# Delta rule on one core: key scaling after the value scaling, eight attention tiles, and loads at other places of SyncE's order

## The chip, the cores and the metric

The kernel runs on one core of a Trainium2 chip. The metric is the device time of one execution in microseconds: 3272.89 us is the median of three runs of the kernel before (3272.14 to 3275.28). The core has TensorE (PE: matmuls, and PEld for its weight loads), VectorE (DVE), ScalarE (ACT), GpSimd (POOL), and SyncE (SP), which here only issues transfers. Each engine works through its own instructions in the order in which they are written, and waits at an instruction until the semaphores it names have reached their values.

## The reference, cut to what matters

Two transformer layers. The change lies in the first one's attention, a gated delta rule over 1024 tokens, 2 sequences, 16 key heads and 32 value heads of 128:

```
q, k, v = silu(conv4(hidden @ W_qkvz));  q, k = l2norm(q) / sqrt(128), l2norm(k)
for each token:                       # per sequence and value head
    S = S * exp(g)
    delta = (v - k @ S) * beta
    S = S + outer(k, delta)
    o = q @ S
out = norm(o * silu(z)) * norm_w @ W_out
```

All else (the routed feed-forward layer before it in the program, the second layer after it) is untouched.

## The kernel before

`delta_rule` computes the scan in chunks of 128 tokens. One *step* is one key head and one chunk, for both sequences and both value heads of the key head (U = 4 units): 16 heads by 8 chunks, 128 steps. Within a chunk the triangular system of the delta rule is solved through the inverse of a 128 by 128 matrix, which is built from inverses of 16 by 16 blocks on GpSimd (`base_start`, `base_row`), doubled on TensorE.

The steps run in a software pipeline. A *slot* is one pass through `body` on each engine; in slot s an engine works on step s minus a lag for each function: `S_P` = 0 (projections, convolution), `S_S` = 1 (SiLU), `S_F` = 2 (keys' transposes, decay matrix, N, attention), `S_L` = 5, `S_D` = 6 (state, solve, apply), `S_E` = 7 (output). `t.c` is the chunk of a step, s its number, so an even slot has even `t.c` at lag 0. The functions of a slot stand in a fixed order written out by hand in each engine's `body`, and none is skipped over: a wait in one holds all that stand behind it on that engine. Between engines only semaphores order the work.

What the text below speaks of, by engine:

- ScalarE: `ztanh`, `expo` (L878, the decay matrix ET from rowb), `norms`, `silu`, `from_state`, `normed` (L963, output scaled, waits for GpSimd's `out_scale`), `xev64` (L933), `wev64` (L941), `kdec` (L888, keys scaled into kd), `vscale` (L900, values scaled into vb), `evac(0)`, `clamp` (L866, Relu on rowb for the next slot's `expo`), `evac(1)` (L923, L924), `gtev`, `squares`.
- TensorE, in this order: keys' transposes, state, `w3`, `x16` (reads Tp), `causal`, `w1` (reads Wp), `x64` (L607), first half of projection 0, `w64` (L620, waits for `xev64`), `w2`, `solve` (L710, waits for `wev64`), second half of projection 0, `values` (L659), `apply` (L721 with kd, L724 with attn), projection 1 (L681, waits for `vscale` of this slot, which frees its bank), `gated_tp`, `zproj`, `project_out`.
- VectorE: among others `strict` (L1138, N), `uscale`, `attention` (L1151), `update`, `output`, `taps` (L1193).
- GpSimd: `step_gates`, `causal` (L417), `derive` (L401 to L408), `halo`, `base_rest` (even slots: rows 6 to 14 of the block inverses), `base_first` (odd slots: `base_start` L459, then rows 1 to 5 by L471 and L475), `out_scale` (L442 to L450).
- SyncE: `decays` (L304, loads rowb, once this slot's `expo` has read the old one), `weights`, `base_out` (even slots: blk_t, blk_w out, Tp, Wp back in), `dump` (L346 writes N to DRAM; in odd slots it then waits for that write and issues L351, the load of Bk, the blocks that `base_start` of the same slot waits for).

kd, attn, N and vb are rings of four tiles. So `kdec` of step s-2 overwrites the kd of step s-6, which is read in this very slot by L721, and waits for it. `attention` stands in the same relation to L724:

```
wait(act, up_mm, t.done(RING))     # kdec
wait(dve, au_mm, t.done(RING))     # attention
```

In `base_start` the wait for Bk, with `read` the count of all loads up to this pair of steps:

```
read, sent = held(pool, t.pairs(16, 16)), held(pool, t.pairs(16))
pool.wait_ge(m["made"], 2)
pool.wait_ge(blk_in, read)
```

Of the kernel before, what the change touches and what calls it, by code (L numbers as in the profile page):

```python
# [11 lines left out]
P = 128  # L12
# [6 lines left out]
U = 4  # L19
# [89 lines left out]
def delta_rule(nc, ins, m, l2, hd, acc, xn, xnT, gates, rows):  # L109
# [7 lines left out]
    with ExitStack() as ctx:  # L117
# [15 lines left out]
        rowb = [sb(f"rowb{r}", [P, U, P]) for r in range(2)]  # L133
        ET = sb("ET", [P, U, P])
        N = [sb(f"N{r}", [P, U, P]) for r in range(RING)]
        attn = [sb(f"attn{r}", [P, U, P]) for r in range(RING)]
        kd = [sb(f"kd{r}", [P, U, P]) for r in range(RING)]
        vb = [sb(f"vb{r}", [P, U, P]) for r in range(RING)]

# [88 lines left out]
        def held(eng, val):  # L228

            if not isinstance(val, int):  # L230
                eng.to_reg(val)
            return val

        def wait(eng, sem, val):
            if not (isinstance(val, int) and val <= 0):
                eng.wait_ge(sem, val)
# [13 lines left out]
        with nc.Block() as block:  # L250
            @block.sync
            def _(sp):
# [9 lines left out]
                def weights(s):  # L262

                    t = s.back(S_P)
                    if not t.live:
                        return
                    first = t.i is None and t.off < C
                    if t.c == 0 and not first:
                        free = held(sp, t.at(1, -1))
                        sp.wait_ge(m["made"], 2)  # L270
                        wait(sp, y_rdy, free)
                        h = bass.ds(t.head(), 1)
                        sp.dma_start(wkq[:, :, 0:P], wq[:, :, h, P:2 * P]).then_inc(wkq_in, 16)
                        sp.dma_start(wkq[:, :, P:], wq[:, :, h, 0:P]).then_inc(wkq_in, 16)
                        sp.dma_start(ckq[:, 0:1, :], cw[:, bass.ds(t.head(1, HK), 1), :]).then_inc(wkq_in, 16)
                        sp.dma_start(ckq[:, 1:2, :], cw[:, h, :]).then_inc(wkq_in, 16)
                    if t.c == 1 and not first:
                        free = held(sp, t.at(1, -1))
                        sp.wait_ge(m["made"], 2)
                        wait(sp, y_rdy, free)  # L280
                        h = bass.ds(t.head(), 1)
                        sp.dma_start(wv[:], wq[:, :, h, 2 * P:4 * P]).then_inc(wv_in, 16)
                        sp.dma_start(cv[:], cw[:, bass.ds(t.head(2, 2 * HK), 2), :]).then_inc(wv_in, 16)
                    if t.c == 5:
                        free = held(sp, t.at(1, -5))
                        sp.wait_ge(m["made"], 2)
                        wait(sp, z_mm, free)
                        sp.dma_start(wz[:], wq[:, :, bass.ds(t.head(), 1), 4 * P:6 * P]).then_inc(wz_in, 16)
                    if t.c == 7:
                        free = held(sp, t.at(1, -7))  # L290
                        sp.wait_ge(m["made"], 2)
                        wait(sp, out_mm, free)
                        sp.dma_start(wout[:], wo[:, bass.ds(t.head(2), 2), :]).then_inc(wo_in, 16)

                def decays(s):

                    t = s.back(S_F - 2)
                    if not t.live:
                        return
                    free = held(sp, t.done(2))  # L300
                    sp.wait_ge(m["made"], 2)
                    sp.wait_ge(hd["rows_out"], 16)
                    wait(sp, exp_rdy, free)
                    sp.dma_start(rowb[t.c % 2][:].rearrange("p (b v) n -> p b (v n)", b=B),  # L304
                                 rows[t.c, :, bass.ds(t.head(), 1), :].rearrange("b h n -> b (h n)").partition_broadcast(P)
                                 ).then_inc(rowb_in[t.c % 2], 16)

                def base_out(s):

# [27 lines left out]
                def dump(s):  # L337

                    t = s.back(S_F)
                    if not t.live:  # L340
                        return
                    made, read, sent, free = (held(sp, v) for v in (t.done(), t.pairs(16), t.at(16, 16), t.pairs()))
                    sp.wait_ge(m["made"], 2)
                    wait(sp, N_rdy, made)
                    wait(sp, blk_in, read)
                    sp.dma_start(units(nd, U * (t.c % 2), U), N[t.c % RING][:]).then_inc(n_out, 16)  # L346
                    if t.c % 2:
                        sp.wait_ge(m["made"], 2)
                        wait(sp, n_out, sent)
                        wait(sp, base_rdy, free)  # L350
                        sp.dma_start(Bk[:], blocks(nd)).then_inc(blk_in, 16)  # L351

                def body(s):
                    decays(s)
                    weights(s)
                    base_out(s)
                    dump(s)
                pipeline(sp, body)
# [161 lines left out]
            def _(pe):  # L520
# [192 lines left out]
                def apply(s):  # L713

                    t = s.back(S_D)
                    if not t.live:
                        return
                    pe.wait_ge(Us_rdy, t.done())
                    pe.wait_ge(oq_rdy, t.done())
                    for u in range(U):  # L720
                        i = pe.matmul(bU[7][:, u], kd[t.c % RING][:, u, :], Us[:, u, :], start=True, stop=True)  # L721
                    i.then_inc(up_mm, 1)
                    for u in range(U):
                        i = pe.matmul(bU[6][:, u], attn[t.c % RING][:, u, :], Us[:, u, :], start=True, stop=True)  # L724
                    i.then_inc(au_mm, 1)

                def gated_tp(s):
# [81 lines left out]
            def _(act):  # L809
# [174 lines left out]
                def body(s):  # L984
                    ztanh(s)
                    expo(s)
                    norms(s)
                    silu(s)
                    from_state(s)
                    normed(s)  # L990
                    xev64(s)
                    wev64(s)
                    kdec(s)
                    vscale(s)
                    evac(s, 0)
                    clamp(s)
                    evac(s, 1)
                    gtev(s)
                    squares(s)
                    low_rank_ev(s)  # L1000
                    norm_ev(s)
# [3 lines left out]
            def _(dve):  # L1005
# [137 lines left out]
                def attention(s):  # L1143

                    t = s.back(S_F)
                    if not t.live:
                        return
                    dve.wait_ge(ET_rdy, t.done())
                    wait(dve, au_mm, t.done(RING))
                    for b in range(B):  # L1150
                        i = dve.tensor_tensor(attn[t.c % RING][:, 2 * b:2 * b + 2, :], ET[:, 2 * b:2 * b + 2, :],  # L1151
                                              bB[3][:, b, P:].unsqueeze(1).broadcast_to([P, 2, P]), ALU.mult)
                    i.then_inc(attn_rdy, 1)

# [1280 lines left out]
```

## Time and profile before

| | |
|---|---|
| median of three runs | 3272.89 us (3272.14 to 3275.28) |
| profiled execution, its own time | 3272.77 us |
| its span in the profile | 3271.1 us |
| the delta rule's slots in it | 308 us to some 2900 us |
| PE busy | 89% of the span |
| DVE, ACT, POOL busy | 69%, 59%, 45% |
| granted clock of TensorE, mean | 0.98 |

### The profile page before, as it was taken

To read this page: it belongs to the slowest core of one execution; us is meant where nothing else is said; L and a number is where in the kernel's file an instruction comes from. 1 tells how busy PE (TensorE), PEld (TensorE's weight loads), DVE (VectorE), ACT (ScalarE), POOL (GpSimd) and SP (SyncE) were. 2 spreads that over 40 slices of the span, in tenths; PEclk is the share of its full clock that TensorE was granted. 3 is DMA by queue.
4 is the path that set the end of the run, shared out by engine and by line. 5 is a ranking of instruction groups with operands and counts; after the bars stand their busy time and mean duration, and the time that the engine had idled before them with its cause. 6 is when DMAs were issued, how large, how long until landed. Compare 5 with 4: busy or idle time off the path is not lost. (4 is left out here: it accounts for less than half of the span.)

```text
span 3271.1 us, 70683 instructions
## 1 busy us (share of the span) xinstructions
PE 2896.6 (89%) x22765; PEld 2135.2 (65%) x22765; DVE 2260.8 (69%) x4805; ACT 1916.4 (59%) x6436; POOL 1482.7 (45%) x3616
## 2 busy tenths in 40 slices
PE   5998689898989898989998899989898989877998
PEld 4555367666766676766666666666676667664555
DVE  3443677777777777777777777777777777645776
ACT  3322566666666666666666666666666666632322
POOL 1000555555555555555555555555555555610000
PEclk8999799999999999999999999999999999988999
DMA  3001222222222222222222222222222222201000
GB/s 81 1 1 23 45 64 50 55 52 52 54 52 51 51 52 53 55 50 55 48 55 48 57 51 61 51 59 48 56 50 56 48 54 48 42 9 39 7 7 13
DMA packets 482423, 147.47 MB, mean 45 GB/s; under 512 B 352592, under 2 KB 481216, under 8 KB 482048
## 3 DMA queue, kind: packets, MB, share of 16 engines
q1 hardware_dynamic: 482048, 142.81, 20.6%
q8 instruction: 194, 3.18, 0.4%
q14 instruction: 181, 1.48, 0.1%
HBM read 97.40 MB, written 45.35 MB: 44 GB/s over the span
## 5 line engine op out<-in xcount | busy, mean ns | idle before, releaser
L888 ACT ACTIVATE kd<-bank,gs 128x128 f32<-128x128 f32 x512 | 146.3, 368 | 442.4 <-PE bank L721 442.4
L681 PE MATMUL bank<-xnT,wkq 128*128 128x512 f32 x512 | 269.6, 631 | 119.6 <-ACT vb L900 85.5
L475 POOL TENSOR_TENSOR Tb<-Tb,btmp 64x14 f32<-64x14 f32 (+6 forms) x896 | 324.9, 363 | 70.2
L681 PE MATMUL bank<-xnT,wv 128*128 128x512 f32 x512 | 263.8, 618 | 103.3 <-ACT vb L900 85.4
L471 POOL TENSOR_TENSOR btmp<-Bk,Tb 64x14 f32<-64x14 f32 (+6 forms) x896 | 302.8, 338 | 65.6
L459 POOL TENSOR_SCALAR Tb<-Bk 64x256 f32<-64x256 f32 x64 | 71.8, 1122 | 553.9 <-DMA Bk<-blk_n 553.9
L1193 DVE SCALAR_TENSOR_TENSOR conv<-raw,ckq,conv 128x512 f32<-128x512 f32 x384 | 279.2, 755 | 20.2 <-ACT conv L924 12.3
L1193 DVE SCALAR_TENSOR_TENSOR conv<-raw,cv,conv 128x512 f32<-128x512 f32 x384 | 280.7, 762 | 12.9 <-ACT conv L924 5.8
L1151 DVE TENSOR_TENSOR attn<-ET,bank 128x256 f32<-128x256 f32 x256 | 96.3, 418 | 263.6 <-PE bank L724 263.6
L750 PE MATMUL bank<-wout_h,gT 128*128 128x256 f32 x1024 | 256.1, 393 | 0.1
L698 PE MATMUL bank<-wz_h,xnT 128*128 128x256 f32 x1024 | 243.8, 381 | 0.0
L533 PE MATMUL bank<-S,ykq 128*128 128x256 f32 x1024 | 242.2, 379 | 0.0
L750 PEld LDWEIGHTS bank<-wout_h,gT 128*128 128x128 f32 x1024 | 185.7, 191 | 49.0 <-ACT gT L951 28.5
L698 PEld LDWEIGHTS bank<-wz_h,xnT 128*128 128x128 f32 x1024 | 185.6, 191 | 21.1 <-issue 1.0
L533 PEld LDWEIGHTS bank<-S,ykq 128*128 128x128 f32 x1024 | 184.7, 190 | 19.8
L681 PEld LDWEIGHTS bank<-xnT,wkq 128*128 128x128 f32 x512 | 84.8, 194 | 171.3 <-issue 145.8
L1124 DVE TENSOR_TENSOR Us<-bank,ty 128x512 f32<-128x512 f32 x128 | 88.6, 692 | 150.1 <-PE bank L710 150.1
L442 POOL TENSOR_TENSOR ty<-ty 128x4 f32<-128x4 f32 x128 | 26.5, 207 | 361.9 <-ACT sq_gat L911 361.9
L681 PEld LDWEIGHTS bank<-xnT,wv 128*128 128x128 f32 x512 | 82.7, 190 | 151.8 <-issue 140.9
L710 PE MATMUL bank<-R,Wf 128*128 128x128 f32 x1024 | 145.5, 285 | 34.1 <-ACT Wf L941 34.1
L417 POOL TENSOR_TENSOR ET<-ET,le 128x512 f32<-128x512 f32 x128 | 163.0, 1273 | 24.0 <-ACT ET L878 24.0
L963 ACT ACTIVATE gatn<-gat,ty 128x128 f32<-128x128 f32 x512 | 167.3, 434 | 6.5 <-POOL ty L450 6.3
(353 smaller groups left out, 7713.0 us busy)
## 6 DMA issues: line engine op xcount, KB each, us to landing
rowb<-decay_rows SPq DMA_DIRECT2D x128, 256.0 KB, 5.0
blk_n<-N SPq DMA_DIRECT2D x128, 256.0 KB, 2.9
Tp<-blk_t SPq DMA_DIRECT2D x128, 128.0 KB, 2.9
Wp<-blk_w SPq DMA_DIRECT2D x128, 128.0 KB, 3.1
wkq<-in_L_attn_W_qkvz_dram SPq DMA_DIRECT2D x32, 128.0 KB, 4.3
wv<-in_L_attn_W_qkvz_dram SPq DMA_DIRECT2D x16, 256.0 KB, 4.4
Bk<-blk_n SPq DMA_DIRECT2D x64, 64.0 KB, 2.7
blk_t<-Tb SPq DMA_DIRECT2D x64, 64.0 KB, 2.5
```

What stands on the lines that cost most here:

```text
L417: pool.tensor_tensor(ET[:], ET[:], le4[:], ALU.mult).then_inc(ET_rdy, 1)
L471: pool.tensor_tensor(tmp, Bk[:, j, j + 1:].unsqueeze(2).broadcast_to([64, 15 - j, j]), Tb[:, j, 0:j].unsqueeze(1).broadcast_to([64, 15 - j ...
L475: pool.tensor_tensor(Tb[:, j + 1:, 0:j], Tb[:, j + 1:, 0:j], tmp, ALU.subtract).then_inc(row_rdy, 1)
L533: i = pe.matmul(bB[6 + j][:, b], chunk(kq_of(t), t, j, b), S[:, 2 * b:2 * b + 2, :].rearrange("p v n -> p (v n)"), start=True, stop=True)
L681: i = pe.matmul(bank[1 - j][:], w[:, k, j * P:(j + 1) * P], xnT[:, k, q * 512:(q + 1) * 512].rearrange("p (c b n) -> p b c n", c=2, b=B), ...
L698: i = pe.matmul(bB[1][:, b], xnT[:, k, n * P:(n + 1) * P], wz[:, k, :], start=(k == 0), stop=(k == KT - 1))
L710: i = pe.matmul(bU[6][:, u], Wf[:, u, :], R[:, u, :], start=True, stop=True)
L750: i = pe.matmul(bB[0][:, h], gT[:, 2 * h + v, :], wout[:, v, :], start=(v == 0), stop=(v == 1))
L888: i = act.activation(kd[t.c % RING][:, u, :], bU[2][:, u // 2], ACT.Copy, scale=gs[t.c][:, DEC, u:u + 1])
L963: i = act.activation(gatn[:, u, :], gat[:, u, :], ACT.Copy, scale=ty[t.c][:, SC, u:u + 1])
L1151: i = dve.tensor_tensor(attn[t.c % RING][:, 2 * b:2 * b + 2, :], ET[:, 2 * b:2 * b + 2, :], bB[3][:, b, P:].unsqueeze(1).broadcast_to([P, ...
L1193: dve.scalar_tensor_tensor(out=conv[h][:, j], in0=raw[h][:, j, :, k:k + 256], scalar=cw[:, j, k:k + 1], in1=conv[h][:, j], op0=ALU.mult, o ...
```

## The change

Three things are stated and one goes with them:

1. ScalarE's order: `clamp` stands where `kdec` stood, ahead of `vscale` and `evac(0)`; `kdec` stands where `clamp` stood, behind them.
2. attn becomes a ring of eight (C = 8), so that `attention` no longer waits for L724 of this slot, only for that of an earlier one.
3. The load of the value weights leaves `weights`, and is issued a slot earlier by `value_weights`, in slots whose chunk is 0.
4. The load of Bk leaves `dump`. `base_load` issues it, for step s-3 in place of s-2, between `weights` and `base_out` of the next slot, an even one. GpSimd's code is unchanged.

```diff
-        attn = [sb(f"attn{r}", [P, U, P]) for r in range(RING)]
+        attn = [sb(f"attn{r}", [P, U, P]) for r in range(C)]
...
-                    if t.c == 1 and not first:
-                        free = held(sp, t.at(1, -1))
...
+                def value_weights(s):
+
+
+                    t = s.back(S_P - 1)
+                    if not t.live or t.c != 1 or (t.i is None and t.off < C):
+                        return
+                    free = held(sp, t.at(1, -1))
+                    sp.wait_ge(m["made"], 2)
+                    wait(sp, y_rdy, free)
+                    h = bass.ds(t.head(), 1)
+                    sp.dma_start(wv[:], wq[:, :, h, 2 * P:4 * P]).then_inc(wv_in, 16)
+                    sp.dma_start(cv[:], cw[:, bass.ds(t.head(2, 2 * HK), 2), :]).then_inc(wv_in, 16)
...
                     sp.dma_start(units(nd, U * (t.c % 2), U), N[t.c % RING][:]).then_inc(n_out, 16)
-                    if t.c % 2:
-                        sp.wait_ge(m["made"], 2)
-                        wait(sp, n_out, sent)
-                        wait(sp, base_rdy, free)
-                        sp.dma_start(Bk[:], blocks(nd)).then_inc(blk_in, 16)
+
+                def base_load(s):
+
+                    t = s.back(S_F + 1)
+                    if not t.live or t.c % 2 == 0:
+                        return
+                    sent, free = held(sp, t.at(16, 16)), held(sp, t.pairs())
+                    sp.wait_ge(m["made"], 2)
+                    wait(sp, n_out, sent)
+                    wait(sp, base_rdy, free)
+                    sp.dma_start(Bk[:], blocks(nd)).then_inc(blk_in, 16)
 
                 def body(s):
                     decays(s)
                     weights(s)
+                    base_load(s)
+                    value_weights(s)
                     base_out(s)
                     dump(s)
...
-                        i = pe.matmul(bU[6][:, u], attn[t.c % RING][:, u, :], Us[:, u, :], start=True, stop=True)
+                        i = pe.matmul(bU[6][:, u], attn[t.c][:, u, :], Us[:, u, :], start=True, stop=True)
...
-                    kdec(s)
+                    clamp(s)
                     vscale(s)
                     evac(s, 0)
-                    clamp(s)
+                    kdec(s)
                     evac(s, 1)
...
-                    wait(dve, au_mm, t.done(RING))
+                    wait(dve, au_mm, t.done(C))
                     for b in range(B):
-                        i = dve.tensor_tensor(attn[t.c % RING][:, 2 * b:2 * b + 2, :], ET[:, 2 * b:2 * b + 2, :],
+                        i = dve.tensor_tensor(attn[t.c][:, 2 * b:2 * b + 2, :], ET[:, 2 * b:2 * b + 2, :],
```

## Rows read from the trace of the kernel before

**Rows 1.** TensorE's waits, 400 to 2800 us: total us, times, longest us.

```profile
PE bank L681 <- ACT vb L900: 169.3, 111, 1.5
...
PE bank L681 <- DMA ckq<-in_L_attn_conv_w_dram: 12.7, 15, 1.4
```

**Rows 2.** Timeline, odd slot: start us, us, engine, line, operation [idle before].

```profile
1604.44 0.65 ACT L878 ACTIVATE ET<-rowb 128x512 f32<-128x512 f32 x1
...
1612.53 0.38 ACT L941 ACTIVATE Wf<-bank 64x256 f32<-64x256 f32 x1 [1.28 <-PE bank L620]
...
1614.88 0.60 PE L659 MATMUL bank<-ident,yv 128*128 128x128 f32 x4
...
1615.40 0.58 SPq L351 DMA_DIRECT2D Bk<-blk_n  x1
...
1616.20 1.06 PE L724 MATMUL bank<-Us,attn 128*128 128x128 f32 x8
1616.47 1.14 ACT L888 ACTIVATE kd<-bank,gs 128x128 f32<-128x128 f32 x4 [3.56 <-PE bank L721]
...
1617.48 1.16 ACT L900 ACTIVATE vb<-bank,ty 128x128 f32<-128x128 f32 x4
...
1618.25 1.07 POOL L459 TENSOR_SCALAR Tb<-Bk 64x256 f32<-64x256 f32 x1 [8.17 <-DMA Bk<-blk_n]
...
1618.79 1.96 PE L681 MATMUL bank<-xnT,wv 128*128 128x512 f32 x4 [1.52 <-ACT vb L900]
...
1619.53 1.34 ACT L866 ACTIVATE rowb<-rowb,gs 128x128 f32<-128x128 f32 x4
```

**Rows 3.** Timeline, the even slot behind it, same columns.

```profile
1624.20 0.64 ACT L878 ACTIVATE ET<-rowb 128x512 f32<-128x512 f32 x1
...
1625.07 0.37 SPq L304 DMA_DIRECT2D rowb<-decay_rows  x1
...
1625.65 0.19 POOL L442 TENSOR_TENSOR ty<-ty 128x4 f32<-128x4 f32 x1
...
1627.39 0.20 POOL L450 TENSOR_TENSOR ty<-ty 128x4 f32<-128x4 f32 x1
...
1628.17 1.31 ACT L963 ACTIVATE gatn<-gat,ty 128x128 f32<-128x128 f32 x4
...
1630.62 0.38 ACT L933 ACTIVATE Xs<-bank 64x256 f32<-64x256 f32 x1 [1.14 <-PE bank L607]
...
1631.57 0.50 PE L620 MATMUL bank<-Wf,Xs 64*64 64x64 f32 x5
...
1635.03 0.27 POOL L471 TENSOR_TENSOR btmp<-Bk,Tb 64x50 f32<-64x50 f32 x1
...
1638.30 0.61 POOL L495 COPY Wb<-Tb 64x256 f32<-64x256 f32 x1
```

**Rows 4.** DMA view, 400 to 2800 us: issues, KB each, median us to landing.

```profile
rowb<-decay_rows SPq DMA_DIRECT2D x120, 256.0 KB, 5.0
...
Bk<-blk_n SPq DMA_DIRECT2D x60, 64.0 KB, 2.7
...
wz_h<-in_L_attn_W_qkvz_dram SPq DMA_DIRECT2D x15, 256.0 KB, 5.5
...
cv<-in_L_attn_conv_w_dram SPq DMA_DIRECT2D x15, 4.0 KB, 4.5
```

**Rows 5.** Timeline of SyncE in a slot whose chunk is 0.

```profile
1704.45 0.37 SPq L304 DMA_DIRECT2D rowb<-decay_rows  x1
...
1706.74 0.34 SPq L276 DMA_DIRECT2D ckq<-in_L_attn_conv_w_dram  x1
```

**Rows 6.** Timeline of TensorE in the first slots.

```profile
362.77 3.75 PE L681 MATMUL bank<-xnT,wkq 128*128 128x512 f32 x4 [5.51 <-issue]
```

**Rows 7.** The same by 1 us: us, PE busy, granted clock, DMA share, GB/s.

```profile
362.00:363.00 1.00, 0.23 (x1) 0.50 0.00 0
...
367.00:368.00 1.00, 0.38 (x2) 0.66 0.00 0
```

More of the change, by code:

```diff
@@ L276, in weights @@
                         sp.dma_start(ckq[:, 1:2, :], cw[:, h, :]).then_inc(wkq_in, 16)
-                    if t.c == 1 and not first:
-                        free = held(sp, t.at(1, -1))
-                        sp.wait_ge(m["made"], 2)
[L280 to L283, printed above, removed]
                     if t.c == 5:
@@ L341, in dump @@
                         return
-                    made, read, sent, free = (held(sp, v) for v in (t.done(), t.pairs(16), t.at(16, 16), t.pairs()))
+                    made, read = held(sp, t.done()), held(sp, t.pairs(16))
                     sp.wait_ge(m["made"], 2)
@@ L346, in dump @@
                     sp.dma_start(units(nd, U * (t.c % 2), U), N[t.c % RING][:]).then_inc(n_out, 16)
-                    if t.c % 2:
-                        sp.wait_ge(m["made"], 2)
-                        wait(sp, n_out, sent)
-                        wait(sp, base_rdy, free)
-                        sp.dma_start(Bk[:], blocks(nd)).then_inc(blk_in, 16)
+                def base_load(s):
[7 more added lines that the diff above has]
+                    sp.dma_start(Bk[:], blocks(nd)).then_inc(blk_in, 16)
                 def body(s):
```

## The prediction, on record before the changed kernel ran

> **What bounds the kernel now.** I read the waits of TensorE first, then the timeline of one odd and one even slot, then SyncE's and GpSimd's part of it, since the change moves two transfers in SyncE's order. TensorE is busy 89% of the span. In the slots one wait of its own stands out: L681, projection 1, waits for `vscale` 111 times, 1.5 us each [rows 1]. The timeline shows why [rows 2]: ScalarE is through with `wev64` at 1612.91, then idles 3.56 us until L721 has read the old kd, does `kdec` (1.14) and `vscale` (1.16), and TensorE starts at 1618.79 what it could have started at some 1617.2, where L724 ends. Slots follow each other every 19.76 us (`expo` starts at 1604.44 in the odd slot and at 1624.20 in the even one [rows 2, 3]); the end of the even slot's `expo`, 1624.84, I call T. So TensorE's own work and this wait make the slot. GpSimd seems off the path, but only just: in the even slot its `out_scale` ends at T+2.75 and ScalarE comes to `normed` at T+3.33 [rows 3]. In odd slots it waits 8.17 us for Bk, which costs nothing there, and the five rows of `base_first` behind that wait fill it until 1625.65, past T [rows 2, 3].
>
> **Part 1, ScalarE's order and attention's ring: a gain.** `clamp` needs nothing from TensorE. It runs in the 3.56 us of idleness: 1612.91 to 1614.25 (1.34). `vscale` then waits only for L659, over at 1615.48: it ends at some 1616.8, where it ended at 1618.64 [rows 2]. L681 starts right behind L724, at 1617.2: 1.6 us earlier. `evac(0)` (0.9 from `vscale`'s end to the next instruction, 1618.64 to 1619.53) and `kdec` (1.14) end at 1618.85, before projection 1 does (1617.2 + 1.96), so `evac(1)`, `gtev` and `project_out` all come 1.6 us earlier too. `kdec` has no reader before the next slots. With the ring of eight, `attention` runs while VectorE would idle, and `update`, `output` and `taps` follow 1.6 us earlier; otherwise they would be next late. TensorE would then be the bound, with nearly no wait left. Slots that have both L724 and L681 of step s: 6 to 127, 122 of them, so 122 x 1.6 = 195 us. By bounds: not under the wait itself, 1.5; not over 1.64, where L724's end is taken as the limit.
>
> **Part 2, value weights.** Two issues move from odd slots to the even slot with chunk 0, behind a wait for `silu` of that slot, ahead of `base_out`. The latter waits for GpSimd's rows there, much later, so nothing is held. The moved wait is worth a few tenths of a us per head.
>
> **Part 3, the load of Bk: a loss, and the largest term.** GpSimd's `base_first` still stands in the odd slot, ahead of `out_scale` of that slot, and needs the load that SyncE now issues in the even slot, behind `decays`, and `decays` waits for `expo` of the even slot. Queued behind L459 on GpSimd: rows 1 to 5, `out_scale`, `step_gates`, `causal`, `derive`. For `out_scale` waits ScalarE's `normed` in the even slot, and behind it `xev64`, for which TensorE's `w64` waits, `wev64`, `solve` and all the rest. Step by step from T:
> - L304 is issued at T+0.23 [rows 3]. One issue takes its place some 0.6 us later, so the load of Bk is issued at T+0.85.
> - It took 2.7 us to land when it was issued alone; rowb takes 5.0, and transfers issued right behind rowb landed in 4.5 (cv) to 5.5 (wz) [rows 4]. Bk now stands right behind rowb. I take 4.5, and 2.7 and 5.5 as bounds. L459 starts 0.15 later (15.40 + 2.7 + 0.15 = 18.25 in [rows 2]): T+5.5.
> - `base_start` (1.07, and 0.3 for a fill behind it) and five rows took 7.40 from L459 to `out_scale` [rows 2, 3], so the rows 6.0. That was beside VectorE's `taps`. Rows of the same sizes in `base_rest` took 3.27 (1635.03 to 1638.30 [rows 3]), before `taps` began. Bounds 4.7 and 7.4; at the new place VectorE has one long SiLU and then waits itself for `derive`, so I take 5.3: `out_scale` starts at T+10.8.
> - `out_scale` takes 1.94 (1625.65 to 1627.59 [rows 3]): T+12.75; `normed` at T+12.85, and `xev64` 1.31 later at T+14.15. It stood at T+5.78 [rows 3]. All behind it comes 8.4 us later. The bounds give 6.0 (2.7 and 4.7) and 11.5 (5.5 and 7.4).
> - `derive`, and N on VectorE behind it, come as much later as `out_scale`. N stands ahead of `uscale` on VectorE, but `uscale` has to wait for `solve` anyway, which is as late. I price this at nothing; a wait of VectorE for L408 longer than that for L710 would show it wrong. `base_rest`, Tp and Wp come later by about as much as the next slot that reads them.
> - In the even slot with chunk 0, four issues of key weights stand between: the last at 1706.74, 2.29 behind L304, where the second issue would stand at 0.6 [rows 5]. One pair of slots in four loses about 2.2 more: 0.5 a pair. There the wait for ckq (12.7 us in 15 [rows 1]) and cv's vanish in the stall: 0.3 a pair back.
>
> The Trainium skill, *DMA: Bandwidth & Descriptors*, section Queues, rings and completion order, says that each DMA engine takes the descriptors of one ring in order. By that rule Bk's would start only behind rowb's, and 2.7 would be out; the trace's 4.5 for the small cv says the same. With 2.7 the stall would be 6.6 and not 8.4 us. *GPSIMD Engine Reference*, section Specifications, has GpSimd share its SBUF interfaces with VectorE when the latter has two inputs there; the five rows' 6.0 us beside `taps` against 3.27 agree, and by that rule 5.3 is nearer than 7.4.
>
> **Part 4, TensorE's clock.** TensorE comes to `w64` at T+6.7 (1631.57 [rows 3]) and now stands until T+15.1 (`xev64` at T+14.15 and the same 0.95 behind it as in [rows 3]). No slot of before has such a gap, but the stage's first slots have: behind 5.51 us of idleness L681 ran at half clock, 1.2 GHz, four matmuls in 3.75 us where 1.96 is usual [rows 2, 6], and the clock was back at 2.4 GHz within the stretch 367 to 368 [rows 7], 4.9 us after the start at 362.77. Half of 4.9 us of dense work is lost: 2.5 us. The work behind `w64` is TensorE's own, without a wait of note, so I charge 2.5 in full. Bounds: nothing, if the clock holds, and some 3, since this gap is half as long again as that one.
>
> **The sum.** A pair of slots loses 8.4 + 2.5 + 0.5 - 0.3 = 11.1 us to the late Bk. 64 loads; the first two pairs lie before the first `normed`: 62 x 11.1 = 688 us. Less 195 us: +493. On the profiled 3272.77 us that is 3766 us, and as the median of the runs is 3272.89, it is the forecast for that too: 3765 us, +15%.
>
> **The rivals.**
> - *The clock holds.* The gap of 8.4 us is then all: 62 x 8.6 - 195 = +338, 3611 us. For it: `w2` and `solve` come at once behind the gap. Against it: 5.5 us of idleness cost the clock in the first slots, and this gap is longer.
> - *The stall is deeper.* GpSimd's rows stay as slow as beside `taps` and Bk lands as late as wz: 62 x (11.5 + 2.5 + 0.2) - 195 = +685, 3958 us. For it: rowb's 256 KB and 1,024 small pieces of Bk together. Against: VectorE is idle then.
> - *The load is hidden, and the kernel is faster.* If Bk came early enough, only part 1 would be left: 3272.8 - 195 = 3078 us. The point from which it decides: GpSimd has 0.58 us to spare in even slots, less 1.6 from part 1, so the load must be issued before T by some 10 us, as it was. It needs SyncE's wait for `expo` to be an old one. The timeline shows it fresh: L304 follows `expo`'s end by 0.23 us [rows 3]. I see no other way to it, and leave it for an error in my reading.
>
> **How the numbers follow.** Forecast 0.6, clock holds 0.2, deeper stall 0.13, hidden 0.05, and 0.02 for something between that moves nothing. The measurement of this kernel can tell some 0.2% from no change: faster 0.05, same 0.01, slower 0.94. The likeliest case's own range, from the landing (1.0 either way) and the rows (up to 2.1), is 3640 to 3860. With the first rival, and part of the second, the range is 3540 to 3880.
>
> **What the profile after would show.** Right: GpSimd's L459 waits some 18 to 20 us for Bk in place of the 8.17 shown, ScalarE's `normed` (L963) waits about 9 us for L450 in every even slot, TensorE's L620 about 8, and its clock falls to half in every pair; odd slots of about 18.1 us and even ones of about 29. L681 no longer waits for L900, nor L888 for L721. Wrong: L351 issued well before `expo` of its slot, or L459 starting before T, would end the argument; a clock of 1.00 throughout would take part 4 away; a wait of TensorE at L550 for Tp would be one that I have priced at nothing.

## The result, and the profile after

The changed kernel takes 3658.99 us (3657.90 to 3664.56, 4 runs) where the kernel before takes 3273.48 us in the same series (4 runs): a ratio of 1.118 (1.116 to 1.120). It is 12% slower, and the forecast was 3765 us (range 3540 to 3880). The profiled execution took 3659.43 us, its span 3657.7.

The page of the profile shows a smaller busy share of every engine, and a lower clock. First the busy times, then the granted clock of TensorE in 40 slices of the span, in tenths (9 is 0.9 or more):

```profile
PE 3005.4 (82%) x22765; PEld 2238.3 (61%) x22765; DVE 2257.8 (62%) x4805; ACT 1932.3 (53%) x6436; POOL 1316.4 (36%) x3616
...
PEclk9997899888998889999988999888888898997999
```

TensorE was busy 89% of the span before and is 82% now, though its busy time grew by 109 us (2896.6 before), since the same matmuls last longer at half clock. The mean granted clock fell from 0.98 to 0.90. Of the 31 slices that lie wholly in the slots 17 now read 8, where before all but the first read 9. Line numbers have moved by 14: L892 is `expo`, L297 `decays`, L363 `base_load`, L473 `base_start`, L456 to L464 `out_scale`, L977 `normed`, L947 `xev64`, L634 `w64`, L724 `solve`, L914 `vscale`, L902 `kdec`, L880 `clamp`, L695 the projections, L738 attention's apply, L1127 SiLU, L1152 N, L564 `x16`.

The timeline of an even slot, start and duration in us, shows the stall from one `expo` to the next [rows 3]:

```profile
1631.62 0.64 ACT L892 ACTIVATE ET<-rowb 128x512 f32<-128x512 f32 x1
...
1632.49 0.37 SPq L297 DMA_DIRECT2D rowb<-decay_rows  x1
...
1633.05 0.58 SPq L363 DMA_DIRECT2D Bk<-blk_n  x1
...
1637.91 1.22 DVE L1127 SCALAR_TENSOR_TENSOR yv<-yv,conv 128x1024 f32<-128x1024 f32 x1
...
1637.96 2.10 POOL L473 TENSOR_SCALAR Tb<-Bk 64x256 f32<-64x256 f32 x1 [18.36 <-DMA Bk<-blk_n]
...
1643.48 0.20 POOL L456 TENSOR_TENSOR ty<-ty 128x4 f32<-128x4 f32 x1
...
1645.22 0.20 POOL L464 TENSOR_TENSOR ty<-ty 128x4 f32<-128x4 f32 x1
...
1645.45 1.28 ACT L977 ACTIVATE gatn<-gat,ty 128x128 f32<-128x128 f32 x4 [9.71 <-POOL ty L464]
...
1646.75 0.38 ACT L947 ACTIVATE Xs<-bank 64x256 f32<-64x256 f32 x1
...
1647.23 0.76 PE L634 MATMUL bank<-Wf,Xs 64*64 64x64 f32 x5 [8.16 <-issue]
...
1648.87 2.04 PE L724 MATMUL bank<-R,Wf 128*128 128x128 f32 x8
...
1649.35 1.12 DVE L1152 SCALAR_TENSOR_TENSOR N<-ET,ty,bank 128x128 f32<-128x128 f32 x4 [10.22 <-POOL ty L422]
...
1650.95 0.69 DVE L1138 TENSOR_TENSOR Us<-bank,ty 128x512 f32<-128x512 f32 x1 [0.48 <-PE bank L724]
...
1660.27 0.65 ACT L892 ACTIVATE ET<-rowb 128x512 f32<-128x512 f32 x1
```

T is 1632.26 here. Bk is issued right behind rowb, at T+0.8, GpSimd stood 18.36 us for it, and `normed` 9.71 us for `out_scale`. `xev64` starts at T+14.49, `w64` at T+15.0 (before: T+5.78, T+6.7 [rows 3]). N, behind `derive`, ends at 1650.47, half a us ahead of `uscale`: as priced, nothing is lost there. (Over the 60 even slots with the stall this distance lies between 0.07 and 0.95 us.) The next `expo` ends at T+28.66.

The granted clock around it, by 1 us (us, PE busy, granted clock, DMA share, GB/s) [rows 7]:

```profile
1641.00:1642.00 1.00, 0.00 (x0) 1.00 0.00 0
1642.00:1643.00 1.00, 0.00 (x0) 0.89 0.00 0
1643.00:1644.00 1.00, 0.00 (x0) 0.50 0.00 0
...
1652.00:1653.00 1.00, 1.00 (x4) 0.50 0.00 0
1653.00:1654.00 1.00, 1.00 (x11) 0.99 0.00 0
```

TensorE stopped near 1639.1. The clock fell to 1.2 GHz between 1642 and 1643 and was back at 2.4 GHz at 1653.0, 5.8 us after the work began again at 1647.23. `solve` took 2.04 us for eight matmuls in it (1.13 in the odd slot ahead of this one).

An odd slot of after, where the first part of the change shows alone [rows 2]:

```profile
1621.71 0.38 ACT L955 ACTIVATE Wf<-bank 64x256 f32<-64x256 f32 x1 [1.28 <-PE bank L634]
1621.99 1.27 ACT L880 ACTIVATE rowb<-rowb,gs 128x128 f32<-128x128 f32 x4
...
1624.06 0.60 PE L673 MATMUL bank<-ident,yv 128*128 128x128 f32 x4
...
1624.70 1.14 ACT L914 ACTIVATE vb<-bank,ty 128x128 f32<-128x128 f32 x4 [1.44 <-PE bank L673]
...
1625.39 1.06 PE L738 MATMUL bank<-Us,attn 128*128 128x128 f32 x8
...
1626.28 1.88 PE L695 MATMUL bank<-xnT,wv 128*128 128x512 f32 x4
...
1626.76 1.18 ACT L902 ACTIVATE kd<-bank,gs 128x128 f32<-128x128 f32 x4
```

`clamp` fills what was idleness, `vscale` waits for L673 only, and projection 1 (1626.28) follows L738 with no wait. TensorE's waits, 400 to 2800 us [rows 1], and ScalarE's first one:

```profile
PE bank L634 <- issue: 399.5, 51, 8.6
PE bank L724 <- ACT Wf L955: 13.7, 52, 0.3
PE bank L695 <- DMA ckq<-in_L_attn_conv_w_dram: 12.2, 13, 1.5
...
PE bank L564 <- DMA Tp<-blk_t: 1.4, 3, 0.9
```

```profile
ACT gatn L977 <- POOL ty L464: 492.1, 51, 10.5
```

The wait for `vscale` is gone, and one for `w64` has come, 399.5 us in 51 slots. ("issue" stands there, since the profile finds no work of another engine that ended just then. What `w64` waits for by its code is `xev64`.) The landing times [rows 4]:

```profile
Bk<-blk_n SPq DMA_DIRECT2D x64, 64.0 KB, 4.8
...
cv<-in_L_attn_conv_w_dram SPq DMA_DIRECT2D x16, 4.0 KB, 2.3
```

From all 122 slots between 400 us and the end of the rule (start of one `expo` to the start of the next): odd slots 18.02 us on average, even ones 27.98, 46.0 a pair. Before, they were 19.85 and 19.96, 39.8 a pair. The difference, 6.2 us, times 61 pairs is 378 of the 386 us. (60 of the 61 even slots have the stall; the last one, behind the last Bk, has none.)

### The profile page after: what moved, and what is told of

It reads as the page before. It is cut to its first block and busy times, and to the rows that moved or that the text cites. A ratio compares the mean times of both kernels' runs of the same rounds, so it can differ in the third digit from the quotient of the medians.

```text
span 3657.7 us, 70679 instructions
## 1 busy us (share of the span) xinstructions
PE 3005.4 (82%) x22765; PEld 2238.3 (61%) x22765; DVE 2257.8 (62%) x4805; ACT 1932.3 (53%) x6436; POOL 1316.4 (36%) x3616
## 5 line engine op out<-in xcount | busy, mean ns | idle before, releaser
L473 POOL TENSOR_SCALAR Tb<-Bk 64x256 f32<-64x256 f32 x64 | 99.3, 1551 | 1191.7 <-DMA Bk<-blk_n 1173.8
L1152 DVE SCALAR_TENSOR_TENSOR N<-ET,ty,bank 128x128 f32<-128x128 f32 x512 | 143.2, 341 | 610.5 <-POOL ty L422 610.3
L634 PE MATMUL bank<-Wf,Xs 64*64 64x64 f32 x1024 | 110.7, 266 | 473.8 <-issue 471.2
L977 ACT ACTIVATE gatn<-gat,ty 128x128 f32<-128x128 f32 x512 | 165.7, 415 | 579.6 <-POOL ty L464 579.6
L634 PEld LDWEIGHTS bank<-Wf,Xs 64*64 64x64 f32 x1024 | 92.0, 173 | 570.1 <-issue 570.1
L695 PE MATMUL bank<-xnT,wkq 128*128 128x512 f32 x512 | 298.3, 690 | 30.8 <-DMA ckq<-in_L_attn_conv_w_dram 13.8
L914 ACT ACTIVATE vb<-bank,ty 128x128 f32<-128x128 f32 x512 | 146.1, 368 | 283.2 <-PE bank L673 279.3
L695 PE MATMUL bank<-xnT,wv 128*128 128x512 f32 x512 | 259.6, 610 | 5.5 <-issue 5.5
L489 POOL TENSOR_TENSOR Tb<-Tb,btmp 64x14 f32<-64x14 f32 (+6 forms) x896 | 235.3, 263 | 70.2
L485 POOL TENSOR_TENSOR btmp<-Bk,Tb 64x14 f32<-64x14 f32 (+6 forms) x896 | 226.9, 253 | 65.6
L724 PE MATMUL bank<-R,Wf 128*128 128x128 f32 x1024 | 200.4, 357 | 22.2 <-ACT Wf L955 18.3
L1176 DVE SCALAR_TENSOR_TENSOR S<-S,gs,bank 128x128 f32<-128x128 f32 x512 | 143.7, 343 | 109.8 <-PE bank L735 109.8
L724 PEld LDWEIGHTS bank<-R,Wf 128*128 128x128 f32 x1024 | 173.8, 256 | 39.1 <-issue 39.1
L547 PEld LDWEIGHTS bank<-S,ykq 128*128 128x128 f32 x1024 | 184.7, 190 | 19.8
L937 ACT ACTIVATE raw<-bank 128x512 f32<-128x512 f32 x256 | 155.1, 606 | 50.4 <-PE bank L695 50.4
```

What stands on the lines that cost most here:

```text
L485: pool.tensor_tensor(tmp, Bk[:, j, j + 1:].unsqueeze(2).broadcast_to([64, 15 - j, j]), Tb[:, j, 0:j].unsqueeze(1).broadcast_to([64, 15 - j ...
L489: pool.tensor_tensor(Tb[:, j + 1:, 0:j], Tb[:, j + 1:, 0:j], tmp, ALU.subtract).then_inc(row_rdy, 1)
L547: i = pe.matmul(bB[6 + j][:, b], chunk(kq_of(t), t, j, b), S[:, 2 * b:2 * b + 2, :].rearrange("p v n -> p (v n)"), start=True, stop=True)
L634: i = pe.matmul(bG[5][0:64, u], Xs64[64:, u, :], Wf[64:, u, 64:], start=True, stop=True)
L695: i = pe.matmul(bank[1 - j][:], w[:, k, j * P:(j + 1) * P], xnT[:, k, q * 512:(q + 1) * 512].rearrange("p (c b n) -> p b c n", c=2, b=B), ...
L724: i = pe.matmul(bU[6][:, u], Wf[:, u, :], R[:, u, :], start=True, stop=True)
```

## The experiments

Ratios are to the kernel before on the same chip, with 95% intervals. "Slots" are averages over 122, measured as above, odd and even. Lines of code differ by a few between kernels.

| | ratio | median us | odd, even slot us |
|---|---|---|---|
| after | 1.118 (1.116 to 1.120) | 3659 | 18.0, 28.0 |
| e1: load of Bk ahead of `decays` | 0.968 (0.966 to 0.969) | 3163 | 19.8, 18.6 |
| e2: ScalarE's order and the ring alone | 0.980 (0.976 to 0.985) | 3212 | 20.5, 18.4 |
| e3: SyncE's part alone | 1.179 (1.177 to 1.181) | 3853 | 19.7, 29.5 |
| e4: gap filled, 28 matmuls | 1.173 (1.170 to 1.175) | 3829 | 18.0, 30.5 |
| e5: gap filled, 14 matmuls | 1.129 (1.127 to 1.131) | 3693 | 20.3, 26.0 |
| e6: e1, three rows in odd slots | 0.979 (0.977 to 0.981) | 3207 | 20.5, 18.2 |
| e7: e1, ring of four | 0.973 (0.971 to 0.975) | 3185 | 19.0, 19.3 |
| e8: load between `decays` and `weights` | 1.112 (1.110 to 1.114) | 3640 | 18.0, 27.7 |
| e9: e1, mask on VectorE | 0.952 (0.951 to 0.954) | 3114 | 19.1, 18.2 |
| e10: e9, three rows in odd slots | 0.954 (0.952 to 0.956) | 3122 | 19.1, 18.2 |
| e11: e5, mask on VectorE | 1.089 (1.086 to 1.092) | 3558 | 18.1, 26.1 |

### e1: the load of Bk ahead of `decays`

```diff
                 def body(s):
+                    base_load(s)
                     decays(s)
                     weights(s)
-                    base_load(s)
                     value_weights(s)
```

> The changed kernel with one call moved: base_load stands ahead of decays in SyncE's order and not behind weights. It is still a function of the next slot. My theory (what costs is that the load of Bk stands behind the wait for expo, so that GpSimd's base_first, out_scale and ScalarE's normed come late): L363 is issued again about 10 us before T (the end of the even slot's expo), the gap of TensorE ahead of w64 and the half clock are gone, and the gain of ScalarE's order is left. Not the whole of it: the slot is 1.76 us shorter, N and with it the load stand where they stood in the odd slot, base_first takes 7.4 us beside the taps, so out_scale ends at about T+4.5 and normed, ready at T+3.3, waits some 1.2 us in every even slot. Odd slots 18.0, even ones 19.3, 2.5 us less for a pair than before: about 3120 us (3100 to 3140). Rival 1 (the order within SyncE is of no account, the lag of a slot is): 3650 us, as the changed kernel. Rival 2 (GpSimd has room to spare once the load is early): two slots of 18.0, about 3050 us.

Measured 3163 us, ratio 0.968. One call moved by two places takes some 490 us away (0.150 of 3273), so the place behind the wait for `expo` is the loss, and "a slot later" is not. Rival 1 is out, and rival 2 too. The timeline:

```profile
1606.42 0.37 SPq L352 DMA_DIRECT2D blk_n<-N  x1
...
1610.33 0.58 SPq L363 DMA_DIRECT2D Bk<-blk_n  x1
...
1613.10 1.50 POOL L473 TENSOR_SCALAR Tb<-Bk 64x256 f32<-64x256 f32 x1 [11.01 <-DMA Bk<-blk_n]
...
1615.80 0.64 ACT L892 ACTIVATE ET<-rowb 128x512 f32<-128x512 f32 x1
...
1619.17 0.19 POOL L456 TENSOR_TENSOR ty<-ty 128x4 f32<-128x4 f32 x1
...
1621.14 1.28 ACT L977 ACTIVATE gatn<-gat,ty 128x128 f32<-128x128 f32 x4 [1.23 <-POOL ty L464]
```

Bk is issued 5.5 us ahead of `expo`'s start (8.8 before), and `normed` waits 1.2 us, as worked out (1621.14 for 1619.17 and the 1.9 of `out_scale`). But 3120 was expected, 3140 at most. ScalarE's wait, and one of TensorE that I had not counted:

```profile
ACT gatn L977 <- POOL ty L464: 41.2, 56, 1.2
```

```profile
PE bank L564 <- DMA Tp<-blk_t: 76.6, 48, 3.8
```

The wait of `normed` costs next to nothing: `xev64` starts at T+5.81 on average in the even slots, for T+5.78 before, since ScalarE would otherwise wait for L621 there (1.14 us for L607 in [rows 3]). The even slots, 18.6, are shorter than the 19.3 expected. The odd ones are longer, 19.8 for 18.0. `x16` waits for Tp in 48 odd slots, and behind the longer of these waits the clock falls: half clock touches 15 of the 61 odd slots, and one even slot. Tp comes through N, Bk, two turns of GpSimd and two transfers. The forecast's part 3 took it as moving with the next slot, which was right with a slow even slot. With both slots short it is late. (The profiled execution took 3182.6 us, the slowest of the five; the other four took 3160 to 3165. Its waits and slots may be somewhat longer than theirs.)

### e2: ScalarE's order and the ring of eight alone

```diff
-                    kdec(s)
+                    clamp(s)
                     vscale(s)
                     evac(s, 0)
-                    clamp(s)
+                    kdec(s)
                     evac(s, 1)
```

and the four lines of attn; SyncE as before.

> The kernel before with ScalarE's new order and the ring of eight alone; SyncE as it was. My theory: as with the load of Bk put ahead of decays, and 5 us more, because TensorE's waits for cv (5.4 us in all before) stay: about 3125 us. Rival 1 (the new order of ScalarE is itself a loss): over 3273 us. Rival 2 (the value weights' load, a slot ahead, carries part of the gain): 20 us or more above the kernel with base_load ahead of decays.

Measured 3212 us, 0.980 (0.976 to 0.985), its runs between 3184 and 3217. The new order is a gain by itself, but of some 2%, 55 to 65 us, and not of the 195 us of the forecast. Rival 1 is out. Rival 2's sign is there: 49 us above e1, not 5. TensorE's waits and SyncE's issues of one slot with chunk 1:

```profile
PE bank L550 <- DMA Tp<-blk_t: 47.1, 32, 3.9
PE bank L681 <- DMA cv<-in_L_attn_conv_w_dram: 47.1, 15, 4.3
```

```profile
1537.19 1.37 SPq L334 DMA_DIRECT2D Wp<-blk_w  x2
...
1539.48 0.39 SPq L304 DMA_DIRECT2D rowb<-decay_rows  x1
1540.11 0.37 SPq L282 DMA_DIRECT2D wv<-in_L_attn_W_qkvz_dram  x1
1540.69 0.37 SPq L283 DMA_DIRECT2D cv<-in_L_attn_conv_w_dram  x1
```

TensorE's waits for cv grew from 5.4 us in 15 to 47.1 in 15, up to 4.3 each. `base_out` of the even slot now reaches past the slot's end (Wp until 1538.6), so `decays` and the value weights behind it are issued late. The value weights' load a slot ahead takes that away. I had priced it at a few tenths of a us a head. The slots themselves show more: the 15 odd slots in which cv is awaited take 23.8 us on average here and 18.6 in the profile of e1, 78 us in all, and two thirds of the half clock of the slots lie in them. The waits for Tp go the other way (47.1 us in 32 here, 76.6 in 48 in e1): the other slots are together 45 us shorter than in e1. 78 less 45 is the 33 to 35 us that lie between the two profiled executions. The place of Bk's load differs between the two as well, so the value weights' share is read from the slots and was not run apart.

### e3: SyncE's part alone

The changed kernel with the old order of ScalarE and the ring of four (the diff of e2 turned round).

> The changed kernel with ScalarE's old order and the ring of four: only SyncE's part is left. My theory, from the parts measured in the two traces: in the even slot xev64 comes at T+14.4 and not at T+5.8, and the half clock costs 1.5 us: a pair takes 39.5 + 8.7 + 1.5 = 49.7 us, about 9.9 us more than before on 62 pairs: about 3880 us (3850 to 3900). Rival 1 (ScalarE's new order takes part in the loss, and without it the late load costs less): below 3800 us. Rival 2 (the two parts don't add, since kdec's old wait now lies under the gap): about 3770 us.

Measured 3853 us, 1.179; pairs of 49.3 us where 49.7 were expected. Both rivals are out. Beside the late load the first part is worth what was forecast: e3 less the changed kernel is 194 us, and the forecast had 195. But the two parts don't add in general. Alone, ScalarE's order and the ring give 0.980 and SyncE's part 1.179, together 1.159 by addition, and the changed kernel has 1.118. In the changed kernel the slow even slot covers Tp, and the value weights come early; in e2 neither is so. SyncE's part alone costs 586 us (3853 less 3268 of the kernel before in that series), where the forecast had 688: that is nearly the whole of its error.

### e4 and e5: TensorE's gap filled

```diff
+                    if s.off(0) % 2 == 0:
+                        wait(pe, w3_rdy, done)
+                        wait(pe, w1_rdy, next_w1)
+                        pe.wait_ge(m["made"], 2)
+                        for _ in range(28):
+                            pe.matmul(bank[5][64:, 256:], m["ident"][:, 0:64],
+                                      le4[:, 0:2, :].rearrange("p u n -> p (u n)"), start=True, stop=True)
                     pe.wait_ge(m["made"], 2)
                     wait(pe, xs64_rdy, done)
```

> The changed kernel with 28 more matmuls (64 rows by 256 columns, of constant tiles, into a quarter of bank 5 that nothing reads) on TensorE in every even slot, ahead of w64, where it stands idle for 8.2 us. They take some 0.24 us each at full clock, 6.6 us in all, so they end before xev64 comes, and change nothing but TensorE's idleness. My theory (of the even slot's time 1.5 us is the half clock that the gap brings): the granted clock is 1.00 through the slots, the even slot takes 26.6 and not 28.2 us, 62 x 1.5 = 93 us less than the changed kernel: about 3565 us. Rival (the clock costs nothing, the 1.5 us are other waits): 3655 us or above. Rival 2 (the fill overruns the gap): an even slot longer than 28.2 us, and L634 without idleness before it.

Measured 3829 us. Rival 2: the fill overran. Each matmul runs as two of 0.22 us, 28 take 12.3 us:

```profile
1606.64 12.30 PE L634 MATMUL bank<-le,ident 128*64 128x256 f32 x56
1618.88 0.50 PE L641 MATMUL bank<-Wf,Xs 64*64 64x64 f32 x5
```

The clock stayed up though (half for 106 us in the whole run, 706 in the changed kernel), and from `w64`'s start to the next slot's transposes it took 11.0 us in this slot, as in the odd slots; it took 13.4 in the slot of the changed kernel shown above. So the next run was the same with 14 (`range(14)`).

> The fill of TensorE's gap again, with 14 matmuls in place of 28: the one with 28 showed that such a matmul runs as two of 0.22 us, so that 28 took 12.3 us and overran the gap of 8.2. 14 take 6.1 us. My theory (1.5 us of the even slot are the half clock): no half clock in the slots, the way from xev64 to the next expo as long as in the odd slots (12.2 us, where the changed kernel has 13.7), even slots of about 26.6 us, 62 x 1.5 = 93 us less than the changed kernel: a ratio to before of about 1.09. Rival (the clock costs nothing, the 1.5 us are other waits): 1.118 as the changed kernel. Rival 2 (the 2 us that stay open are enough to bring the clock down): clock as in the changed kernel.

Measured 3693 us, 1.129: slower than the changed kernel. The even slots did as expected, 26.0 on average and many 25.2 to 25.4. From `xev64` to the end of the next `expo` they take 12.2 us, as the odd ones do, for 13.7 in the changed kernel: 1.5 us is what the half clock cost. The other 0.5 is an `xev64` that comes at T+13.8 for T+14.3. What they gave back was lost in the odd ones, 20.3 for 18.0, and more:

```profile
PE bank L564 <- DMA Tp<-blk_t: 78.5, 43, 5.2
PE bank L641 <- issue: 57.1, 49, 2.1
```

The slow even slot had been Tp's cover (10.4 us of waits in the whole run of the changed kernel). With it gone, `x16` waits 1.8 us on average and up to 5.2, and behind the long ones the clock falls again in the odd slot: half clock touches 22 of the 61. No theory had that.

### e11: the same, with Tp early

ET's mask goes from GpSimd, where it stands ahead of `derive` and `base_rest`, to VectorE:

```diff
                     dve.wait_ge(exp_rdy, t.done())
+                    dve.tensor_tensor(ET[:], ET[:], le4[:], ALU.mult).then_inc(ET_rdy, 1)
+                    dve.wait_ge(ET_rdy, t.done())
                     dve.wait_ge(der_rdy, t.done())
```

> The changed kernel (base_load behind weights) with the 14 filling matmuls in TensorE's gap and the mask on VectorE. With the fill alone the even slots fell from 28.0 to 26.0 us on average, most of the rest at full clock to 25.3, but the odd ones rose from 18.0 to 20.3, since Tp, which had been covered by the slower even slot, came late. My theory (the half clock costs about 2 us in an even slot, and what it gave back was lost to Tp): with Tp 1.3 us earlier odd slots fall below 19, even ones stay under 26: 62 x (46.0 - 44.3) = 105 us less than the changed kernel, a ratio of 1.085, and below the fill alone (1.129) in any case. Rival (the fill itself costs, for instance by its weight loads or its place ahead of w64): odd slots stay near 20 without a wait for Tp, ratio 1.12 or more.

Measured 3558 us, 1.089: 101 us less than the changed kernel, odd slots 18.1, even 26.1.

```profile
PE bank L640 <- issue: 77.3, 51, 2.1
...
PE bank L563 <- DMA Tp<-blk_t: 5.4, 7, 2.3
```

The rival is out: with Tp on time the odd slots are back at 18.1 with the fill in place. 101 us by 61 is 1.7 a pair: the way from `xev64` to the next `expo`'s end is down to 12.0, and `xev64` comes 0.2 sooner. The mask's own share in that was not run apart, so e5's 1.5 is the cleaner price of the half clock.

### e6, e9, e10: what is left in e1

e6 is e1 with `base_row` 4 and 5 done in `base_rest`:

```diff
-                    for j in range(1, 6):
+                    for j in range(1, 4):
...
-                    for j in range(6, ROWS + 1):
+                    for j in range(4, ROWS + 1):
```

> The kernel with base_load ahead of decays, and on GpSimd rows 4 and 5 of the block inverses moved from base_first (odd slots) to base_rest (even slots). It speaks to what is left in that kernel: 1.2 us of waiting of ScalarE's normed in even slots, and a wait of TensorE's x16 for Tp in the odd ones (86 us in 51). Theory A (the two waits are one latency, from N to Tp through GpSimd, and work moved within it only changes which wait shows it): normed waits no more, x16 waits longer, about 3150 us, a ratio of 0.964 where that kernel has 0.968. Theory B (they are separate): 61 x 1.2 = 75 us less, a ratio of 0.945.

Measured 3207 us, 0.979, where theory A had 0.964 and theory B 0.945. Theory B is out. `normed` waits no more, `x16` waits longer.

```profile
ACT gatn L977 <- POOL ty L464: 0.4, 2, 0.2
```

```profile
PE bank L564 <- DMA Tp<-blk_t: 100.0, 45, 4.5
```

The wait of `normed` had cost nothing in e1, so nothing was gained with it: `xev64` stands at T+5.78 in the even slots, for T+5.81. The two rows are now done in the even slot, and Tp comes later by them: the odd slots rose from 19.8 to 20.5.

e9 is e1 with the mask on VectorE:

> The kernel with base_load ahead of decays, and the multiplication of ET by the mask (1.27 us on GpSimd in every slot, ahead of derive and base_rest) done by VectorE just ahead of strict, where it waits for solve anyway. What is left in the kernel with base_load first is a latency through GpSimd: TensorE's x16 waits for Tp in 48 odd slots, 76 us in all, 3.8 at most, with the clock falling behind the longer ones. My theory: base_rest ends 1.3 us earlier, most waits for Tp go, the 1.2 us wait of normed in even slots stays: odd slots of 18.2 in place of 19.8, about 3080 us, a ratio of 0.94. Rival (VectorE becomes late: 0.7 us more a slot ahead of uscale): slots above 19 and a wait of TensorE for Us; ratio 0.97 or more.

Measured 3114 us, 0.952. It is the fastest of all, 4.8% faster than before and 15% faster than the changed kernel, though 3080 was expected: the odd slots fell to 19.1 and not to 18.2. The rival is out. Waits for Tp are down from 76.6 to 46.0 us:

```profile
PE bank L563 <- DMA Tp<-blk_t: 46.0, 48, 3.9
```

e10 is both:

> The same with rows 4 and 5 of the block inverses in base_rest. Moved alone they took the wait of normed away, but made x16 wait longer (48 waits, 116 us) and the clock fall: 1.1% slower than without. With the mask gone from GpSimd, Tp has 1.3 us more. My theory (one latency): between, no better than with the mask moved alone, 3080 to 3130 us, a ratio of 0.94 to 0.955. Rival (the 1.3 us are enough for both waits): all slots 18.0, 3045 us, 0.93.

Measured 3122 us, 0.954, no better than e9, as the first theory had it, and its rival is out. The traces give another reason than one latency, though. From e9 to e10 the waits of `normed` go (57.9 us in 62 in e9), those for Tp stay as they were (45.6 us), and the slots stay at 19.1 and 18.2: the wait of `normed` was off the path, as in e1. What is left in e9 is the wait for Tp. The half clock lasted 141 us in e9, 184 in e1 and 245 in e6: it follows the waits for Tp.

### e7: the ring of four

e1 with attn's four lines as before.

> The kernel with base_load ahead of decays, with attention's ring back at four. attention then waits for L738 again (0.75 us of work that comes after it and not before), and update, output and the taps behind it come up to 1.5 us later than with the ring of eight, in a slot that is 1.76 us shorter. My theory: the taps end after the next slot has begun, rhs and SiLU are late by 0.5 us or so, and the ring of eight is worth 0.3 to 0.7 us a slot: 40 to 85 us more, a ratio of 0.98 to 0.994. Rival (VectorE has slack enough): 0.968 as with the ring of eight.

Measured 3185 us, 0.973 (0.971 to 0.975) for e1's 0.968 (0.966 to 0.969): the ring of eight is worth some 20 us, 0.5%, less than the 40 us expected, and more than the rival's nothing.

```profile
PE bank L749 <- DVE gat L1188: 109.3, 119, 0.9
...
PE bank L564 <- DMA Tp<-blk_t: 2.0, 1, 2.0
```

The slots take 19.0 and 19.3 us, so the later VectorE (`gated_tp` waits for `output`) costs some 1.0 a slot. But such slots are long enough for Tp, which waits 2.0 us in all. The one wait replaces the other. (The 20 us lie between the medians; e1's profiled execution was as long as this one, so the two traces don't show them.)

### e8: the load between `decays` and `weights`

```diff
                     decays(s)
-                    weights(s)
                     base_load(s)
+                    weights(s)
```

> The changed kernel with base_load between decays and weights, so that in slots with chunk 0 the four issues of key weights stand behind it and no longer ahead of it: the load of Bk is issued 2.3 us earlier there, in 15 slots. By the forecast's price (0.5 us a pair) 31 us less than the changed kernel, a ratio to before of 1.109. By the trace after, where out_scale starts at T+11.2 whether the load was issued at T+0.8 or at T+3.1: base_start can't end before VectorE's SiLU does, so the 2.3 us are worth 0.1 to 0.3: 1.117, within 0.2% of the changed kernel's 1.118.

Measured 3640 us, 1.112 (1.110 to 1.114): 19 us less, between the two. Even slots take 27.7 us for 28.0. But only part of it is what was meant: the 15 slots with chunk 0 take 28.1 us for 28.5, 7 us in all. The other 45 have the load issued at T+0.8 in both kernels and take 27.8 for 28.0, 13 us in all: `base_start` got in ahead of VectorE's SiLU in 22 of them, for 8 in the changed kernel (what that is worth, see the last section). Why it did so more often is not shown.

## Why the prediction was right, and where its sizes were off

Its steps against the traces, per pair of slots:

- **ScalarE's order and the ring** (forecast 2 x 1.6 = 3.2). An undisturbed odd slot fell from 19.76 to 18.00, so 2 x 1.76. e3 shows 194 us for it beside the late load, the forecast 195. That the number holds there is in part luck: the forecast took the two parts as separate, and e2 shows that without the late load the first is worth some 60 us, since cv and Tp then come late.
- **The late load** (8.4, and 0.5 for chunk 0). `xev64` stands at T+14.3 on average in the even slots of after, at T+5.8 before: 8.5 in place of 8.9. The landing was 4.8 us for the 4.5 taken. Five rows and `base_start` took 4.5 to 4.8 us undisturbed and up to 5.6 with the landing at its usual place, for the 5.3 taken. The term of chunk 0 was wrong as 0.5: the slots with the load issued at T+3.1 have `out_scale` at T+11.2 to 12.0, the others at T+10.0 to 11.7, which makes 0.1 a pair (28.5 and 28.0 us a slot, in one pair of four); e8's slots with chunk 0 say the same, 7 us in all. That the place in SyncE's order is the cause, e1 shows.
- **The half clock** (2.5). This is the term that was mis-sized most. `xev64` to the next `expo`'s end takes 13.7 us in the even slots and 12.2 in the odd ones: 1.5. By e5 it is 1.5 too, by e11, where the mask moved as well, up to 1.7. That the clock falls was right in all 60 even slots with the gap. The length was right too: from `w64`'s start the clock stayed at half for 3.3 to 6.7 us, 4.9 on average, and 4.9 had been read in the first slots. What failed is the step "I charge 2.5 in full". In each of the 60 slots the cost is half of that length less 0.9 us, within 0.1 us: 0.8 where it was 3.5 us, 2.0 in the slot shown (5.8 us; 14.2 for 12.2), 2.4 where it was 6.7. The 0.9 are time that was no dense work: `w64` starts 0.48 us behind `xev64` (1647.23, 1646.75), where it takes 0.95 in the odd slots since TensorE is still at work, and from `w64` to `solve` it waits for ScalarE, 1.64 us at half clock for 1.23.
- **The rows from which the half clock was foreseen.** This reading of the forecast was wrong. The 5.51 us of idleness ahead of L681 in the first slots can't have cost the clock: in the trace of before it falls at 357.4 us, just as this idleness begins at 357.26. What came before was 0.66 us of work from 356.60, behind 3.39 us of idleness. So those rows show what work at half clock takes, and not that this idleness brought it on. That the gap of some 8 us in the slots brings it on, only the run of the changed kernel showed.
- **ckq and cv** (0.3 back). The wait for ckq is still there, 12.2 us in 13, but it lies ahead of the gap and shortens that; cv's is gone. As priced.
- **Tp, Wp and N at nothing.** Right for the changed kernel: 10.4 us of waits for Tp in the whole run, N done before `uscale`, at the least by 0.07 us. e5 shows that this stood on the slow even slot.

The sum: -3.5 + 8.5 + 1.5, less 0.3 of head by head waits that are gone or lie ahead of the gap, is 6.2 a pair, where the forecast had 7.9. Of the 1.7 between them, 1.0 is the half clock, 0.4 the late load and 0.3 the first part. 61 pairs make 378 us and 386 were measured. The rival "the clock holds" (3611) is out by the clock itself, though the time lies nearer to it than to the forecast; "the load is hidden" is out, since Bk is issued at T+0.8 and `normed` waits 9.71 us; "the stall is deeper" too, since GpSimd's rows were fast. The forecast's cause is the right one, and its time, 106 us too long, lies at 2.9% from the measured one.

What stays open: why the clock comes back after 3.3 us of work in some even slots and after 6.7 in others; and what the value weights' load and the mask are worth in the changed kernel, since neither was run apart.

## What to carry to other kernels

A transfer that is moved in a queue's order inherits every wait ahead of it: ask of each wait there when it ends, and who stands in line behind the one that needs the data. Here a load that was due at the end of an odd slot was put behind a semaphore of the next one, and ScalarE, VectorE and TensorE stood for 8 to 10 us in every second slot. Once the main wait is gone, look for the long latency that runs through several engines over two slots: work taken off it (e9) gains, work put off within it (e6) loses. A wait that shows in the profile is worth nothing if the engine would wait for something else right behind it (`normed` in e1). And two gains that are each real need not add: a slow slot covers waits that come up once it is fast (e2, e3, e5).

## What the runs showed of the hardware

- GpSimd's L473, which takes 1.07 us alone, took 2.10 when VectorE's SiLU (two inputs and the output in SBUF, 1.22 us) started first, and ended 0.9 us behind it. Where L473 started at T+5.61 or sooner, `out_scale` came 4.65 us later; where it started between T+5.66 and T+6.8, it came at T+11.2 to 11.3 whatever the start. So 1.1 us of earlier landing were worth nothing, and the next 0.1 were worth 1.0. That SiLU starts at T+5.65 makes the edge. Where L473 got in ahead of it, it was SiLU that took longer, 1.43 to 1.65 us for 1.22. The Trainium skill, *GPSIMD Engine Reference*, section Specifications, has the SBUF interfaces of GpSimd shared with VectorE, and names VectorE's instructions with two SBUF inputs as ones that contend for them. These rows agree.
- cv lands in 2.3 us when it is not issued behind rowb (4.5 behind it [rows 4]), and Bk in 4.8 behind rowb (2.7 alone [rows 4]).
- A stretch at half clock cost the even slot half of its length less 0.9 us: 0.8 us for 3.5 us of it, 2.4 for 6.7, in 60 slots. With 6 us of matmuls on constant tiles put into the gap of 8.2 us (e5) the clock stayed at full in 52 of these slots.
